# A window-attention, convolution and MLP block with its step loop written out, one maximum moved, narrower weights, one masked copy and two taps on POOL

## The reference, cut to what matters

```python
xn = _layernorm(xw, ln_g, ln_b)                       # xw: (2048 windows, 49, 96)
qkv = (xn @ qkv_w.T + qkv_b).reshape(Bw, N, 3, HEADS, HEAD_DIM)
attn = jnp.einsum('bhnd,bhmd->bhnm', q * SCALE, k) + bias
attn = jax.nn.softmax(attn, axis=-1)
out = jnp.einsum('bhnm,bhmd->bhnd', attn, v).transpose(0, 2, 1, 3).reshape(Bw, N, C)
seq = shortcut + (out @ proj_w.T + proj_b)
conv = lax.conv_general_dilated(x_local, conv_w, (1, 1), ((1, 1), (1, 1)), feature_group_count=DIM)
seq2 = (conv - bn_mean) * (bn_g * lax.rsqrt(bn_var + EPS)) + bn_b
h = jax.nn.gelu(seq2 @ w1.T + b1, approximate=False)
seq = seq2 + (h @ w2.T + b2)
```

## Time and profile before

| | |
|---|---|
| median of 3 runs | 3946.48 us |
| lowest and highest | 3935.39 and 3948.78 us |
| the profiled execution's own time | 3944.66 us |
| its span, first to last instruction | 3942.9 us |
| mean granted clock of TensorE | 0.968 |
| instructions | 199136 |

### The profile page before, as it was taken

The page is one execution under the profiler, slowest core; times in us unless marked ns, Lnnn a source line. Parts: engine busy times, 40 slices in busy tenths (PEclk is TensorE's granted clock), DMA queues, the critical chain, the costliest instruction groups (busy, mean ns, idle before and its releaser), DMA issues.

```text
span 3942.9 us, 199136 instructions
## 1 busy us (share of the span) xinstructions
PE 3638.6 (92%) x83724; PEld 2351.4 (60%) x83724; DVE 2947.5 (75%) x5155; ACT 3111.2 (79%) x5123; POOL 1136.0 (29%) x1550
## 2 busy tenths in 40 slices
PE   4999999999999999999999999999999999999998
PEld 2656666656666666655666666565666666666664
DVE  4777777777777778777777777777777777777776
ACT  2878887778877778877788787787778887787886
POOL 2322322232322223232223232322222332222232
PEclk9999999999999999999999999999999999999999
DMA  1222322222222222222223222222222222222221
GB/s 48 85 87 79 89 83 83 80 84 81 87 86 80 82 84 87 79 87 78 84 82 89 80 86 78 87 87 80 81 83 80 87 87 79 86 80 83 85 86 53
DMA packets 269552, 322.52 MB, mean 82 GB/s; under 512 B 55123, under 2 KB 252180, under 8 KB 268662
## 3 DMA queue, kind: packets, MB, share of 16 engines
q1 hardware_dynamic: 235894, 232.12, 20.5%
q0 software_dynamic: 32768, 77.14, 6.0%
HBM read 39.35 MB, written 38.54 MB: 20 GB/s over the span
## 4 chain that ended last, share of the span: by engine, by line
PE 75%; ACT 11%; DVE 7%; issue 6%; SPq 1%; DMA 0%; POOL 0%; DVEq 0%; POOLq 0%; ACTq 0%
PE a_ps L443 14%; PE sm_ps L327 10%; PE o_ps L344 7%; PE a_ps L362 6%; PE a_ps L435 5%; PE st_ps L312 5%; DVE mx L678 5%; PE b_ps L435 5%; PE d_ps L354 4%; PE d_ps L435 4%; PE b_ps L285 4%; ACT sq L566 4%; ACT sq L568 3%; ACT sq L562 3%; PE b_ps L287 2%
## 5 line engine op out<-in xcount | busy, mean ns | idle before, releaser
L700 DVE SCALAR_TENSOR_TENSOR s<-ximg,cols,s 96x392 f32<-96x392 f32 x2048 | 1260.5, 615 | 21.3 <-POOL s L602 2.9
L678 DVE TENSOR_REDUCE mx<-sm_ps 128x12 f16<-128x588 f32 x1024 | 781.6, 763 | 597.1 <-PE sm_ps L327 597.1
L602 POOL TENSOR_TENSOR s<-ximg,cols 96x392 f32<-96x392 f32 x256 | 215.9, 844 | 2563.9 <-DVE y L731 2563.9
L504 ACT ACTIVATE p<-st_ps 128x588 f32<-128x588 f32 x1024 | 670.8, 655 | 132.0 <-PE st_ps L312 125.9
L327 PEld LDWEIGHTS sm_ps<-k_all,q_all 127*64 127x64 f16 x24576 | 486.1, 115 | 332.7 <-issue 236.4
L443 PE MATMUL a_ps<-g,w_s 128*96 128x392 f32 x1536 | 635.8, 525 | 0.0
L327 PE MATMUL sm_ps<-k_all,q_all 127*64 127x49 f16 x24576 | 595.0, 194 | 6.1 <-DMA q_all<-ql 4.9
L609 POOL DMA_DIRECT2D ox<-o_sb x1024 | 582.9, 572 | 44.1 <-issue 30.3
L312 PEld LDWEIGHTS st_ps<-q_all,k_all 128*64 128x64 f16 x24576 | 483.3, 114 | 152.5 <-issue 148.5
L312 PE MATMUL st_ps<-q_all,k_all 128*64 128x49 f16 x24576 | 569.4, 192 | 0.5 <-issue 0.5
L344 PE MATMUL o_ps<-p,v 128*32 128x49 f32 x24576 | 432.4, 212 | 134.2 <-DVE mx L678 132.7
(11 more groups left out here) (98 smaller groups left out, 5607.1 us busy)
## 6 DMA issues: line engine op xcount, KB each, us to landing
ox<-o_sb POOLq DMA_DIRECT2D x1024, 73.5 KB, 2.6
k_all<-kh SPq DMA_DIRECT2D x512, 96.0 KB
q_all<-qh SPq DMA_DIRECT2D x512, 96.0 KB
x_sb<-in_x SPq DMA_DIRECT2D x256, 147.0 KB, 2.4
out<-y SPq DMA_DIRECT2D x256, 147.0 KB, 2.9
k_all<-kl SPq DMA_DIRECT2D x256, 96.0 KB
q_all<-ql SPq DMA_DIRECT2D x256, 96.0 KB
q_all<-mxt SPq DMA_DIRECT2D x256, 12.0 KB, 2.0
```

The source lines that it names most:

```text
L504: af(p32[:, q, :, :].rearrange("p (b h) n -> p b h n", b=2), st_ps[:, :, 0:HALF].rearrange("p b (h n) -> p b h n", n=TOK), ACT.Exp).then_i ...
L678: v.tensor_reduce(mx[:, (st[1] - lag) % 2, :, p].rearrange("p (b h) -> p b h", b=2), sm_ps[:, :, 0:HALF].rearrange("p b (h n) -> p b h n", ...
L700: v.scalar_tensor_tensor(acc, image_rows(st, lag, k // 3, k % 3), cw_c[:, k:k + 1], acc, ALU.mult, ALU.add)\
```

## The change

- The hardware loop goes: all 264 steps are issued as straight code.
- The fourth block of `max_scores` moves on PE from behind the projection to behind the centring, and DVE's fourth `maxima` from behind `xn` to ahead of the last tap. `keys` moves ahead of the second block of `max_scores`.
- Both kinds of scores load 49 weight columns instead of 64; rows 49 to 63 and 113 to 127 of the score banks are cleared once at the start.
- One DVE instruction writes both value words of `v32`: `b_ps`, each element read twice, times a mask `half_c` that is 1/256 for the right window's half and 0 elsewhere. It stands ahead of `y`. ACT's instruction and the wait for it go.
- POOL makes taps 0 and 1: two products by a scalar (`tensor_scalar`), and an addition of the two. DVE begins with tap 2, in the following step.

```diff
         def run(eng, step):
 
-            for e in range(UN):
-                step((0, e))
-            with eng.Fori(1, CHUNKS // UN - 1) as u:
-                for e in range(UN):
-                    step((u, e))
-            for s in range(CHUNKS - UN, STEPS):
-                step((s // UN, s % UN))
+            for n in range(STEPS):
+                step((n // UN, n % UN))
...
-                        last = mm(st_ps[64 * w:64 * w + 64, h // HH, c0:c0 + TOK], k_all[:, r, h, n:n + WP],
+                        last = mm(st_ps[64 * w:64 * w + TOK, h // HH, c0:c0 + TOK], k_all[:, r, h, n:n + TOK],
...
-                        last = mm(sm_ps[64 * w:64 * w + 64, h // HH, c0:c0 + TOK], q_all[0:MAXROW, r, h, n:n + WP],
+                        last = mm(sm_ps[64 * w:64 * w + TOK, h // HH, c0:c0 + TOK], q_all[0:MAXROW, r, h, n:n + TOK],
...
                 queries(st)
+                keys(st)
                 max_scores(st, 2, 1)
-                keys(st)
...
                 centred(st)
+                max_scores(st, 2, 3)
                 exp_scores(st, 3, 1)
                 variance(st)
                 projection(st)
-                max_scores(st, 2, 3)
                 exp_scores(st, 3, 2)
...
-                if real(st, 2):
-                    wait(act, v_done, st, 2)
-                    wait(act, pv_done, st, 4, NP)
-                    af(v32[0:TOK, (st[1] - 2) % 2, :, :, :].rearrange("p h n (d x) -> p (h n d) x", x=4)[:, :, 0],
-                       b_ps[0:TOK, 0:NP * C], ACT.Identity, scale=1 / UP).then_inc(v32a_done, 1)
...
+                    acc = s2[0:C, st[1] % 2, :].rearrange("c (r q) -> c r q", q=SIDE)
                     wait(pool, sum_done, st, 6)
                     wait(pool, y_done, st, 8)
-                    tt(s2[0:C, st[1] % 2, :].rearrange("c (r q) -> c r q", q=SIDE), image_rows(st, 6, 0, 0),
-                       cw_c[:, 0:1].unsqueeze(2).broadcast_to([C, WS, SIDE]), ALU.mult).then_inc(tap0_done, 1)
+                    wait(pool, tap0_done, st, 7, 3)
+                    pool.sem_inc(turn, 1)
+                    nc.gpsimd.tensor_scalar(acc, image_rows(st, 6, 0, 0), cw_c[:, 0:1], None, ALU.mult).then_inc(tap0_done, 1)
+                    nc.gpsimd.tensor_scalar(t1[:, :].rearrange("c (r q) -> c r q", q=SIDE), image_rows(st, 6, 0, 1), cw_c[:, 1:2], None, ALU.mult)\
+                      .then_inc(tap0_done, 1)
+                    wait(pool, tap0_done, st, 6, 3, 2)
+                    tt(acc, acc, t1[:, :].rearrange("c (r q) -> c r q", q=SIDE), ALU.add).then_inc(tap0_done, 1)
...
+            for t in (st_ps, sm_ps):
+                v.memset(t[:, :, 0:HALF], 0.0)
...
                 tap(st, 7, 7)
+                if real(st, 2):
+                    wait(dve, v_done, st, 2)
+                    wait(dve, pv_done, st, 4, NP)
+                    v.tensor_tensor(v32[:, e % 2, :, :, :].rearrange("p h n (d x) -> p (h n d) x", x=4)[:, :, 0:2],
+                                    b_ps[:, 0:NP * C].unsqueeze(2).broadcast_to([128, NP * C, 2]),
+                                    half_c[:, :].unsqueeze(1).broadcast_to([128, NP * C, 2]), ALU.mult).then_inc(v32_done, 1)
                 if real(st, 8):
...
                      .then_inc(y_done, 1)
-                if real(st, 2):
-                    wait(dve, v_done, st, 2)
-                    wait(dve, pv_done, st, 4, NP)
-                    v.tensor_scalar(v32[64:64 + TOK, e % 2, :, :, :].rearrange("p h n (d x) -> p (h n d) x", x=4)[:, :, 1],
-                                    b_ps[64:64 + TOK, 0:NP * C], 1 / UP, None, ALU.mult).then_inc(v32b_done, 1)
+                maxima(st, 2, 3)
                 tap(st, 7, 8)
...
-                maxima(st, 2, 3)
-                tap(st, 6, 1)
```

More of the change, by code:

```diff
@@ L35 @@
 UP = 256.0
-LOADS = 31
+LOADS = 32
 UN = CPI
 def block_program(nc, x, w_qkv, b_qkv_row, b_v, w_proj, w_proj_rows, b_proj, ln_g, ln_b, bias_q,
-                  conv_w, bn_g, bn_b, bn_mean, bn_var, w1, b1, w2, b2, eye, low, out):
+                  conv_w, bn_g, bn_b, bn_mean, bn_var, w1, b1, w2, b2, eye, low, half, out):
     ctx = ExitStack()
@@ L62, in block_program @@
         low_c = sb("low_c", [ROWS, 1])
+        half_c = sb("half_c", [128, 2])
         g_c, b_c, bv_c, bng_c, bnb_c, bnm_c, bnv_c, b2_c = (cols[:, i:i + 1] for i in range(8))
@@ L83, in block_program @@
         s2 = sb("s2", [97, 2, CT])
+        t1 = sb("t1", [C, CT])
         g = sb("g", [128, NB, CT])
@@ L119, in block_program @@
             "q_done", "k_done", "qh_done", "kh_done", "ql_done", "kl_done"))
-        v_done, v32a_done, v32b_done = sem("v_done"), sem("v32a_done"), sem("v32b_done")
+        v_done, v32_done = sem("v_done"), sem("v32_done")
         sm_done, max_done, mxt_done, mxt_out = sem("sm_done"), sem("max_done"), sem("mxt_done"), sem("mxt_out")
@@ L206, in _ @@
                 (w2_s[:, :, :], w2), (eye_f[:, :], eye),
-                (low_c[:, :], low),
+                (low_c[:, :], low), (half_c[:, :], half),
             ]
@@ L334, in values_times_p @@
                 if q == 0:
-                    wait(pe, v32a_done, st, lag)
-                    wait(pe, v32b_done, st, lag)
+                    wait(pe, v32_done, st, lag)
                 wait(pe, p_done, st, lag, NP, q + 1)
@@ L379, in keys @@
                     wait(pe, kl_done, st, 2)
-                    wait(pe, v32a_done, st, 3)
-                    wait(pe, v32b_done, st, 3)
+                    wait(pe, v32_done, st, 3)
                     wait(pe, sum_done, st, 6)
@@ L405, in projection @@
                 if real(st, 2):
-                    wait(pe, v32a_done, st, 2)
-                    wait(pe, v32b_done, st, 2)
+                    wait(pe, v32_done, st, 2)
                 else:
@@ L419, in hidden @@
                 if k == 0:
-                    wait(pe, tap_done, st, lag, 8)
+                    wait(pe, tap_done, st, lag, 7)
                     if real(st, 0):
@@ L693, in tap @@
                 acc = s2[0:C, (st[1] - lag) % 2, :].rearrange("c (r q) -> c r q", q=SIDE)
-                if k == 1:
-                    wait(dve, tap0_done, st, lag)
+                if k == 2:
+                    wait(dve, tap0_done, st, lag, 3)
                 else:
-                    wait(dve, tap_done, st, lag, 8, k - 1)
+                    wait(dve, tap_done, st, lag, 7, k - 2)
                 if k == 6 and real(st, 6):
@@ L782 @@
         low[row:row + n] = -1.0
+    half = np.zeros((128, 2), np.float32)
+    for w in range(2):
+        half[64 * w:64 * w + TOK, w] = 1 / UP
     col = lambda v: a(v).reshape(C, 1)
@@ L798 @@
         "eye": np.eye(128, dtype=np.float32),
-        "low": low,
+        "low": low, "half": half,
     }
```

## The result

| | before | after |
|---|---|---|
| median | 3946.35 us (5 runs) | 3916.02 us (5 runs, 3911.13 to 3920.37) |
| ratio to before, 95% interval | | 0.9928 [0.9912, 0.9944] |
| profiled span | 3942.9 us | 3914.2 us |
| granted clock, mean | 0.968 | 0.990 |
| instructions | 199136 | 189035 |

The kernel is 30 us faster. The forecast of 3876 had the sign, but the gain is 30 us and not 70: of the 192 us of the loop some 160 are eaten up, not 120. The measured time lies inside the range, outside the likeliest case's own range of 3845 to 3900.

The account below looks back on a forecast made before the run. The prediction took the ring through ACT and DVE, 13.89 + 0.87 = 14.76 us a step, to bound the changed kernel: 3944.7 - 192 (jumps) + 121 (longer step) + 2 (setup) = 3876 us, range 3750 to 3960.

Parts of the forecast that it names:

- the likeliest case: The prediction's own forecast for the whole kernel: 3876 us, own range 3845 to 3900, chance 68%.
- Straight code, -192: Hardware loop: removing its 29 jumps back, with the cold stretches after them, saves 192 us.
- rival (d): Instruction fetch: straight code stalls as often as the loop, giving 4068 us; chance 3%.
- The ring of 13.89: Dependency cycle through ACT, DVE, `y` and PE's variance matmul: 13.89 us a step, 0.38 under today's 14.27.
- 0.87 for the copy in it: Masked copy on DVE ahead of `y`: takes 0.95 us, lengthens the ring by 0.87 to 14.76 a step.
- (a): Rival: the ring isn't the limit; today's step gives 3755 us (5%), PE's step 3441 us (2%).
- (c): Rival on DVE: the masked copy costs 1.66 us, ring 15.47, total 4051 us; chance 7%.
- 49 columns and the order of the last maximum: nothing: PE: they save up to 0.7 and 0.97 us a step, but PE is no longer the bound.
- The tap that DVE loses: nothing: End of DVE's step: one tap of 0.61 us fewer gains nothing, as DVE then waits for the first scores.
- the term P: POOL's two products, one addition and a handoff: 1.6 to 3.1 us, taken as 2.2; POOL's line is 11.5 + P.
- rival (b): POOL becomes the bound from P = 3.2, slower than before from 3.6; at P = 4.0, 4056 us; chance 15%.
- Setup, +2: Start of the kernel: two clears of PSUM and one more load cost about 2 us once.

Follow-up runs that it names:

- `y` first: The changed kernel with `y` moved ahead of the masked copy on DVE: 3784.20 us, ratio 0.9592 to the kernel before.
- the run with 64: The changed kernel with 64 weight columns loaded for the scores as before, instead of 49: 3918.36 us, ratio 0.9932 to the kernel before.
- tap back: The changed kernel with POOL making only tap 0 and DVE making tap 1 as before: 3852.00 us, ratio 0.9767 to the kernel before.
- loop back: The changed kernel with the hardware loop of the kernel before: 4089.97 us, ratio 1.0373 to the kernel before.

## Why the prediction was off, point by point

In terms of the profiled span the forecast was 132.4 + 2 + 247 x 14.76 + 92.9 = 3873; measured were 131.5 + 247 x 14.704 + 51.9 + 98.9 = 3914. The 41 us between them are -14 (the step), +52 (uneven periods), +6 (the end) and -3 (the start and setup).

- *Straight code, -192.* Right: straight code alone gave 189. The rival (d) falls.
- *The ring of 13.89, and 0.87 for the copy in it.* Right within 0.06: 14.704 with the copy, 13.843 without; the difference of 0.86 is the copy's 0.948 less an overlap. Rivals (a) and (c) fall. In the first, (a), the ring would have to have slack; `y` first alone was worth 132 us. The price of (c) was itself somewhat high: by the rows behind the 0.95 the fixed part is 0.16 and not 0.06 us, which makes 1.56 of its 1.66.
- *49 columns and the order of the last maximum: nothing.* Right for the columns, shown by the run with 64. The order wasn't tried by itself, so its worth is argued: the step is set elsewhere.
- *The tap that DVE loses: nothing.* Right; giving it back left the step at 14.706. The premise "DVE itself does not slow down" was true of the trace before only. There the tap beside `xl` began first and took 0.61; in the change it begins 0.20 us behind `xl` and takes 1.15, in 240 steps. With the longer copy of the values it is why DVE's busy time rose from 2947.5 to 2952.9 us with one tap less to do. It cost no time that the trace shows, as DVE waits for PE's scores behind that tap and the next (0.67 us in the step above).
- *POOL.* This step failed: the term P, put at 2.2 us within 1.6 to 3.1. Its bounds for a product, 0.34 and 0.84, were wrong: the low bound came from a MEMSET, the high one from a product in another form of instruction, and the form in the change, `tensor_scalar` with its factor from a column, took 1.26. P was 3.6, above the whole range. The prediction had named this hole (no row showed that form on POOL) and closed it with a row of another form as if it were a ceiling.
- *"It decides from P = 3.2 on", and slower than before from 3.6 on.* The mechanism of rival (b), with the wrong sort of threshold. The usual step did not grow and the kernel did not get slower, by luck: `xl` took 0.92 rather than 1.29, which nothing in the prediction foresaw, and P = 3.6 just fitted. What POOL's line lost was its room. The standstill of 2.5 to 2.8 us once in 31 steps was in the trace of before, one row in POOL's timeline between the tap and the issues, and POOL's line had 2.8 us of room there. Against rival (b) the prediction held POOL's 10.1 us of idle time a step; what counts is the room, 2.8, and the sum has no term for periods that lack it. Behind two taps each standstill cost 4.3 us, the standstill itself and then slow matmuls, 34 us in all, and 18 more lay in the small uneven periods. One tap fewer on POOL removed the 52 us, 9 at the end and 5 at the start.
- *Setup, +2.* The first steady copy came 0.9 us earlier than before, not later.

The small uneven periods go with transfers that land late. Taken one by one, 30 of the 35 that are 0.08 us or more over the usual step, with most of their time (16 us), are periods in which ACT's inverses waited for the transfers; with one transfer on SP it is 16 of 17. They went from 18 to 5 to 0.3 us as one and then two transfers left POOL. No run changed the landing time alone, so that the wait is the cause is likely and not shown. In the run with `y` first only 16 of the 30 small ones have such a wait.

## What to carry to other kernels

Work moved to an engine that looks idle must be priced by the very form of instruction, and against the room that its line leaves in the step, not against its busy share. Before filling an engine's idle gap, look down its whole timeline for rare long gaps of its own: as long as the line has that much room they are free (2.8 us here, of 10 us idle), without it each one cost 4.3 us. And on a ring through several engines the place of an instruction can matter more than its cost: the same masked copy cost 0.86 us a step ahead of `y` and nothing behind it.

## What the runs showed of the hardware

- POOL's product of 96 x 392 float32 by a column took 1.26 us as `tensor_scalar` and 0.84 as `tensor_tensor` with the column broadcast, both with a tap of DVE that starts 0.4 us later. The Trainium skill (GPSIMD Engine Reference, Elementwise — side-by-side cycle accounting) gives about 1.8 cycles an element for its best loop and 2.6 for two inputs; the estimate from them at 1.2 GHz, 0.59 and 0.85 us, agrees for `tensor_tensor` with the two-input figure, and for the one-input `tensor_scalar` it is less than half of what was measured.
- Once in 124 to 126 DMAs that POOL issued, it stood still for 2.35 to 2.8 us ahead of the next, in every kernel here. DMAs issued by SP did not shorten the count.
- Where a tap of DVE and an instruction of POOL overlapped, the one that started second was mostly the longer for it. POOL's, with a tap running at its start or starting within 0.01 us of it: 1.67 instead of 1.25 for the second product, 1.15 instead of 0.83 for its other form, 1.31 instead of 0.90 to 0.92 for `xl`. DVE's tap, when POOL's `tensor_tensor` had begun first: 1.15 instead of 0.61 at 0.20 us behind `xl`, 0.86 at 0.46 behind it (tap back), 0.83 at 0.43 behind the product. A tap 0.25 us behind the start of the `tensor_scalar` product took 0.75 (loop back), and one 0.4 us behind it lengthened nothing (0.62 and 1.26). The Trainium skill (GPSIMD Engine Reference, Specifications) says that POOL and VectorE share their interfaces to SBUF and contend where the latter has two inputs there, as a tap has; the lengthened ones agree with that, the last pair doesn't, and no run separated them. That one waits for the other is inferred from start times and durations.
